# Gat and typed edge passes: the one-hot comparison reads its row of positions from PSUM, and each batch's first four one-hots are built three visits sooner

## The reference, cut to what matters

```python
# layer 0, first pass (gat, 4 heads); layer 1 (typed, 8 heads) adds a type per edge and scales by edge_weight
logits = leaky_relu(a_src[src] + a_dst[dst], 0.2)
m = segment_max(logits, dst); e = exp(logits - m[dst]); s = segment_sum(e, dst)
out = segment_sum(h[src] * (e / s[dst])[:, :, None], dst)
# layer 0, second pass (attn, 1 head): the logit of an edge is q[dst] . k[src] / 16
```

## Time and profile before

| | before |
|---|---|
| median of 3 runs | 4019.19 us (4018.22 to 4026.18) |
| the profiled execution's own time | 4026.38 us |
| its span, first to last instruction | 4024.5 us |
| mean granted TensorE clock | 0.84 of full speed |
| busy: VectorE / PE / GpSimd / ScalarE | 3098.9 / 2979.5 / 2711.6 / 1579.6 us |
| share of the span | 77% / 74% / 67% / 39% |
| first and last gather, gat pass | 144.9 and 1173.6 us |
| first and last gather, attn pass | 1381.4 and 2359.7 us |
| first and last gather, typed pass | 2573.4 and 3587.9 us |

### The profile page before, as it was taken

How to read it: one execution, slowest core, us unless ns; L and a number is a source line. 1 busy time by engine, 2 the same in 40 slices (tenths; PEclk the granted TensorE clock), 3 DMA queues, 4 the chain that set the end, 5 groups by cost and what they waited for, 6 DMA issues and landing times. The chain is left out here.

```text
span 4024.5 us, 71289 instructions
## 1 busy us (share of the span) xinstructions
PE 2979.5 (74%) x14389; PEld 2091.7 (52%) x14389; DVE 3098.9 (77%) x9652; ACT 1579.6 (39%) x5470; POOL 2711.6 (67%) x2963
## 2 busy tenths in 40 slices
PE   5366777777776677788888888466676677777998
PEld 4244444444455455555655556334444444447998
DVE  6467778788887766677777768678888899997886
ACT  2333333333326556566666665311111122212332
POOL 3577777777750277777777735577777777755886
PEclk9666667677778889999999999777777888888999
DMA  4555555566533445554555536555555555533221
GB/s 133 162 158 155 157 164 163 162 173 174 174 108 109 135 136 141 137 138 141 143 139 141 143 93 207 178 146 145 147 145 149 151 152 150 150 100 91 72 73 50
DMA packets 290351, 561.60 MB, mean 140 GB/s; under 512 B 85318, under 2 KB 183278, under 8 KB 289998
## 3 DMA queue, kind: packets, MB, share of 16 engines
q0 software_dynamic: 115872, 326.30, 29.5%
q10 hardware_dynamic: 101462, 168.49, 13.7%
q1 hardware_dynamic: 72664, 63.00, 5.5%
HBM read 479.67 MB, written 77.89 MB: 139 GB/s over the span
## 5 line engine op out<-in xcount | busy, mean ns | idle before, releaser
L481 PE MATMUL psum<-big,onehots_or_distances 128*128 128x264 f32 (+2 forms) x5280 | 1894.8, 482 | 49.7 <-ACT onehots_or_distances L377 38.1
L481 PEld LDWEIGHTS psum<-big,onehots_or_distances 128*128 128x128 f32 x5280 | 1035.9, 228 | 210.3 <-issue 60.8
L281 POOL DMA_INDIRECT big<-table_attn,src_by_edge x782 | 741.3, 948 | 444.8 <-issue 237.9
L281 POOL DMA_INDIRECT big<-table_gat,src_by_edge x782 | 775.0, 991 | 264.9 <-issue 230.0
L281 POOL DMA_INDIRECT big<-table_typed,src_by_edge x782 | 776.7, 993 | 248.1 <-issue 237.3
L683 DVE TENSOR_TENSOR acc<-acc,psum 128x264 f32 (+2 forms) x1320 | 561.0, 425 | 338.1 <-PE psum L481 262.6
L660 DVE TENSOR_TENSOR big<-big,psum 128x512 f32<-128x512 f32 x880 | 595.3, 677 | 10.1 <-issue 0.6
L442 PE MATMUL psum<-big,onehot_t 128*128 x2640 | 466.9, 287 | 146.8 <-SPq L271 94.1
L525 DVE SCALAR_TENSOR_TENSOR dot_products<-psum,big 128x258 f32<-128x258 f32 x880 | 367.1, 420 | 201.6 <-PE psum L442 196.8
L442 PEld LDWEIGHTS psum<-big,onehot_t 128*128 128x128 bf16 x2640 | 262.6, 101 | 353.7 <-issue 239.4
L448 PE MATMUL psum<-big 128*128 128x12 bf16 (+1 forms) x1184 | 134.3, 191 | 419.2 <-ACT big L335 416.9
(11 more groups left out here) (285 smaller groups left out, 4342.3 us busy)
## 6 DMA issues: line engine op xcount, KB each, us to landing
onehot_t<-onehots ACTq DMA_DIRECT2D x73, 512.0 KB, 3.9
big<-visit_positions ACTq DMA_DIRECT2D x55, 512.0 KB
onehots<-big ACTq DMA_DIRECT2D x37, 512.0 KB, 6.0
big<-onehots ACTq DMA_DIRECT2D x37, 512.0 KB
big<-in_x_dram SPq DMA_DIRECT2D x98, 128.0 KB, 2.6
big<-table_gat,src_by_edge POOLq DMA_INDIRECT x782
big<-table_attn,src_by_edge POOLq DMA_INDIRECT x782
big<-table_typed,src_by_edge POOLq DMA_INDIRECT x782
```

What stands on the lines that cost most here:

```text
L281: pool.indirect_dma_start(X[:, t % RING, :], None, ph.table, bass.IndirectOffsetOnAxis(ap=m.src[:, t:t + 1], axis=0)).then_inc(S[f"rows{t ...
L481: last = nc.tensor.matmul(sum_ps(w), onehot_at(v), rows, start=(v % 2 == 0), stop=(v % 2 == 1))
```

## The change

ScalarE copies `m.iota` into columns 384 to 511 of `weight_bank` once, at the start of each gat and typed pass. L648's comparison takes the row from there; its other input, the column of `m.tables`, stays in SBUF. The first comparison of a pass waits for the copy. The comparison for a batch's first four visits moves from v % 16 = 14 to v % 16 = 11 (G - 5), where it stands behind the add and ahead of `shift`; the other three of a batch stay at v % 16 = 2, 6 and 10. Their number (220 a pass), their slots and what they wait for stay as they were.

```diff
--- before.py
+++ after.py
@@ -192,6 +192,7 @@
     raw_weights = ps[:, weight_bank, 0:R].rearrange("p (g h) -> p g h", g=G)
     row_weights = ps[:, weight_bank, P:P + R].rearrange("p (g h) -> p g h", g=G) if ph.typed else raw_weights
     shrink = m.shrink[:, 0:H] if ph.dot else ps[:, weight_bank, 2 * P:2 * P + H]
+    iota = ps[:, weight_bank, 3 * P:4 * P]
     logit_ps = ps[0:R, 6, 0:P]
     max_ps = ps[:, 6, P:P + R]
     grow_ps = ps[:, 6, 2 * P:2 * P + H]
@@ -390,6 +391,8 @@
                 nc.scalar.activation(onehot_t(k), m.rel_row.bitcast(BF16)[:, k % 2, :], ACT.Relu, scale=-1.0, bias=m.ones[:, 0:1]).then_inc(S["onehot_t"], 1)
 
             weigh_at = G - 1 if ph.dot else G - 3
+            if not ph.dot:
+                nc.scalar.activation(iota, m.iota[:, :], ACT.Copy).then_inc(S["iota"], 1)
             places = needs = blks = ()
             for v in range(-5 * G, VISIT_END):
                 transfers(v)
@@ -644,8 +647,10 @@
                     dve.wait_ge(S[f"tables{k % TB}"], (k // TB + 1) * 16)
                 if j >= 3:
                     dve.wait_ge(S["summed"], 2 * (j - 2))
+                if j == 0:
+                    dve.wait_ge(S["iota"], 1)
                 at = 4 * j % ONEHOTS
-                nc.vector.tensor_tensor(m.onehots[:, at:at + 4, :], m.iota[:, :].unsqueeze(1).to_broadcast([P, 4, P]),
+                nc.vector.tensor_tensor(m.onehots[:, at:at + 4, :], iota.unsqueeze(1).to_broadcast([P, 4, P]),
                                         column(k, 0)[:, g:g + 4].unsqueeze(2).to_broadcast([P, 4, P]), ALU.is_equal).then_inc(S["onehots"], 1)
 
             def scale_rows(w):
@@ -712,7 +717,7 @@
                     scale_rows(w + 1)
                 if ph.dot and 0 <= v + DOT_AHEAD < VISIT_END:
                     dot(v + DOT_AHEAD)
-                if not ph.dot and v % 4 == 2 and 0 <= v + 2 < VISIT_END:
+                if not ph.dot and v % 4 == 2 and v % G != G - 2 and 0 <= v + 2 < VISIT_END:
                     onehots((v + 2) // 4)
                 b, g = chain_at(v)
                 for at, place, part in parts:
@@ -722,6 +727,8 @@
                     last_blk, blks = (blks[PAIRS - 1] if k else None), blocks_of(k)
                 if v % 2 and w >= behind:
                     add(w - behind, last_blk if begins else blks[(w - behind) % PAIRS])
+                if not ph.dot and v % G == G - 5 and 0 <= v + 5 < VISIT_END:
+                    onehots((v + 5) // 4)
                 for at, place, part in parts:
                     if b is not None and (at, place) == (g, 1):
                         part(b)
```

## The result

The changed kernel takes 3978.3 us (median of 4 runs, 3972.8 to 3980.6) against 4018.7 us before: ratio 0.9893, 95% interval 0.9881 to 0.9906, 40 us less. Its profiled execution took 3978.11 us with a span of 3976.2, so it lies at the median, where the one before lay 7 us above.

A forecast was written before the change was run, and what follows sets the result against it. GpSimd's almost unbroken stream of gathers, plus the work after the last one, was taken as the bound, VectorE in some stretches; gat 24 + typed 24 = 48 us less, 4019.2 to 3971 us, range 3948 to 4003.

The forecast's parts named there:

- three signs of being wrong: Gathers beside L648 still 1.2 us or more; L648 over 730 ns; VectorE waits ahead of the batch's first L660.
- The row in PSUM frees the gathers: With one comparison input in PSUM, GpSimd's gathers lose their whole excess: 33.6 us in gat, 35.2 in typed.
- The rival in which the second input still holds the gather: Column of m.tables in SBUF alone holds the gather back, nothing is freed, time stays at 4019 us; chance 0.09.
- The comparison costs the same: On VectorE, L648 with one input in PSUM takes as long as before: 0 us, or 2 us either way.
- Gat, 24 us: Gat pass: of GpSimd's excess, 21.1 us in stretches three to five plus 6.3 in the first two, less 3.
- a shorter gather becomes in part a longer wait: Gat's first two stretches: GpSimd waits for ring places VectorE frees, so half counts, 6.3 of 12.7 us.
- Typed, 24 us: Typed pass: 17.1 us from the first three stretches, 6.5 from the fourth, nothing of 9.7 in the fifth.
- after the last gather VectorE has 39.3 and 41.3 us of work left, and nothing of it changes: Ends of gat and typed: VectorE's work behind the last gather, 39.3 and 41.3 us, stays as it was.
- It is the bound there: Typed's fifth stretch: VectorE, busy 193.5 of 206.4 us, is the bound, so nothing of 9.7 us counts.
- The move, 0 us: First four one-hots three visits sooner: VectorE's work is the same, weights 0.60 us later with 0.75 to spare; costs nothing.
- The rival that ends slower: Moved comparison delays what frees the ring and releases the weights: 66 us on top, 4037 us; chance 0.07.
- All of it arrives: GpSimd runs ahead in sparse batches, nothing lost to ring or VectorE: 68.8 us less, 3950 us; chance 0.14.

The follow-up runs named there:

- e2: Kernel before with the row of positions in PSUM in gat alone, first four one-hots at their old place, typed as before: 3992.9 us, ratio 0.9942.
- e7: Changed kernel with the comparison's inputs swapped, column of the tables (SBUF) first, row of positions (PSUM) second: 3988.1 us in its one execution.
- e4: e3 with the load of the batch's block numbers also covered, moved up to v % 16 = 2: 3961.2 us, ratio 0.9850 to the kernel before.
- e3: Changed kernel with VectorE's load of a batch's eight ring places issued at v % 16 = 12, behind L660: 3972.2 us, ratio 0.9881 to the kernel before.
- e1: Kernel before with only the move of the first four one-hots to v % 16 = 11, row still in SBUF: ratio 1.0044.
- e6: e1 with the load of the ring places covered at v % 16 = 12: 4024.9 us, ratio 1.0008 to the kernel before.
- e5: Typed as e4; gat with the row in PSUM's bank 3, first four one-hots at their old place, block-number load covered: 3954.8 us, ratio 0.9835 to the kernel before.
- e8: Changed kernel with gat's L383, ScalarE's absolute distance, cut to 2 of 2048 elements: 3978.1 us in its one execution.

## Why the prediction was right, and where it was off

The forecast was 48 us less, 40 were measured, for the most part by the mechanism that it named. Part of the nearness is luck: in the profiles gat gave 5.2 us more than its 24 and typed 8.9 less. The forecast of 3978.4 for the profiled execution met 3978.11, but that pair has the 7 us in it by which the profile before lay above the median.

Its signs came out unevenly. Mean and longest gather, the comparison's 682 ns and typed's 990.9 us from first to last gather are as it said. Gat's 994.2 us lie below its 1000 to 1008, gat's waits for the ring did not grow, and VectorE in typed's late batches went from 94% busy to 93. And one of its three signs of being wrong is there: VectorE waits ahead of the batch's first scale, 29.1 us in 54 times in gat.

- **The row in PSUM frees the gathers: right, in size too.** 68.8 us were foreseen and 68.0 went; e2 shows it for the row alone and e7 for either order of inputs. The rival in which the second input still holds the gather is out: both of its signs, gathers of 1.2 us beside the comparison and an unmoved mean, are absent.
- **The comparison costs the same: right.** 682 ns before and after. The sum taken from the rows L660 and L525 held. The figure of the Trainium skill (Perfetto Trace Analysis, Optimizing Scalar/DVE Operations) would have made it some 65 ns longer (an estimate from that page); the runs have 682 and 678 ns (e7), so they do not bear it out.
- **Gat, 24 us: 29.2 measured.** The step "a shorter gather becomes in part a longer wait", with half of 12.7 us and 3 more taken off, was wrong. GpSimd's waits for the ring were 24.7 us and are 23.2, and the time from first to last gather fell by 34.5 us, all of the excess and 1.4 more. 5.3 of that came back behind the last gather, from which to the last add it was 39.7 us and is 45.0.
- **Typed, 24 us: 15.1 measured.** From first to last gather 23.6 us went, as forecast. But that is the end of the gathers and not of the pass, and one step that failed is "after the last gather VectorE has 39.3 and 41.3 us of work left, and nothing of it changes": from the last gather to the last add it went from 42.9 to 51.4 us. With GpSimd ahead of VectorE (13.0 of its 18.0 us of ring waits lie in the twelve late batches) the ring is full near the end, and what it holds must be worked off at VectorE's pace. In e4, where GpSimd never waits in those batches, it is 42.9 again. Counted by batches, the first 40 gave 18.8 us, where the first four stretches were to give 23.6; the next twelve took 2.9 more, where nothing was counted either way, and the last three 0.8 more. "It is the bound there" was not quite so either: before, GpSimd set the pace of the twelve at 205.0 us, and VectorE with its load covered could do them in 203.4 (e3).
- **The move, 0 us: wrong, the one step that was not seen.** "What could be late next are the weights" looked at data; they were in time. It was the sequencer: L648 covered `places_of`. The edit was costed at nothing without asking what the moved instruction itself covered. The trace of before had both rows: 32.0 us of "issue" ahead of L683, 0.60 us at a time, behind `blocks_of`, another load of eight registers, and next to nothing ahead of the first scale. Alone the move costs 18 us (e1), and none clear of the noise with the load covered (e6). In the changed kernel covering it gives back 5 us by the ratios and 10 by the profile of typed (e3).
- **The rival that ends slower** stood at the same place, by another mechanism (the weights late), and was priced at 66 us. VectorE's time at the batch's end did grow, by 0.49 us in gat (timeline) and about 0.45 in typed, but e3 gave time back only in typed, where VectorE sets the pace.
- **All of it arrives (3950 us)** did not come, yet e5 comes near with 3954.8 by removing VectorE's load stalls, one of which the kernel before had too.

Open: what makes gat wait for the ring for some 20 us. It is not ScalarE's L383 (e8) and not VectorE's loads (gat gained nothing in e4). Open too is why gat's pass is 2 to 9 us longer with the early place, loads covered or not, when VectorE has idle time there: the direction is the same in all seven profiles, the size is uncertain and the cause not shown.

## What to carry to other kernels

An instruction that reads two SBUF operands on VectorE can lengthen GpSimd's gathers; compare the mean duration of the same gather in a phase that has such an instruction and in one that has none, and put the constant operand into PSUM where a bank is free. Before moving an instruction, look at what its own run time covers, register loads of the engine's sequencer among it, as well as at who waits for it. And count a gain on the engine that leads only up to where another takes over: the end of its stream is followed by all that it has got ahead by.

## What the runs showed of the hardware that was not expected

- A load of eight registers on VectorE costs 0.59 us of idle time when a short instruction stands ahead of it and next to none behind one of 0.68 us (e3, e4): its price goes by what stands ahead of it.
- How much the comparisons lengthen the gathers varies with VectorE's order and its gaps: the same 220 comparisons a pass made typed's gathers 993, 1005 or 988 ns long (before, e1, e6). Two comparisons 0.94 us apart can hold one gather twice: the 35 beside both took 1296 ns on average in e1, those beside one 1127.
- The granted TensorE clock in typed's twelve late batches fell from 0.88 to 0.80, with PE busy for 10.5 us more over a stretch longer by 2.9; in e4 it was 0.82 with the batches 5% shorter. PE was busy for 69 and 73% of the stretch, and VectorE's waits for PE's sums there fell from 6.9 to 1.2 us, so nothing there shows the lower clock setting the pace of these batches.
